# Attention sums over values: high and low parts in one product of six matmuls instead of nine

## The reference

```python
x = x + xattn(_layernorm(x), ctx)      # the part that is changed
x = x + ffn(_layernorm(x))             # top 2 of 8 experts and a shared one

q = (x @ Wq).reshape(b, n, HEADS, DIM_HEAD)
k = (context @ Wk).reshape(b, m, HEADS, DIM_HEAD)
v = (context @ Wv).reshape(b, m, HEADS, DIM_HEAD)
sim = jnp.einsum('bihd,bjhd->bhij', q, k) * SCALE
attn = jax.nn.softmax(sim, axis=-1)
out = jnp.einsum('bhij,bjhd->bihd', attn, v).reshape(b, n, HEADS * DIM_HEAD)
return out @ Wout + bout
```

## Time and profile before

| | |
|---|---|
| median of the timed runs | 1270.85 us |
| profiled execution | 1277.05 us |
| its span | 1275.4 us |
| granted TensorE clock, mean | 0.957 |
| TensorE busy | 1165.7 us (91%) |
| VectorE busy | 748.1 us (59%) |
| ScalarE busy | 671.6 us (53%) |
| GpSimd busy | 802.0 us (63%) |

### The profile page before, as it was taken

One profiled execution on the slowest core, in us unless ns is written; L12 is line 12 of the kernel. 1 busy time (PEld: TensorE's weight loads), 2 busy tenths in 40 slices (PEclk: granted clock), 3 DMA queues, 4 the chain that ended last, 5 costly groups with the idle time before them and its releaser, 6 DMA issues. The chain is left out here.

```text
span 1275.4 us, 27342 instructions
## 1 busy us (share of the span) xinstructions
PE 1165.7 (91%) x7710; PEld 1014.8 (80%) x7710; DVE 748.1 (59%) x2147; ACT 671.6 (53%) x1743; POOL 802.0 (63%) x867
## 2 busy tenths in 40 slices
PE   5989999999999999999998789996989999999792
PEld 4778888888888888888887678885878888888582
DVE  4667787778777877777777456565433333343231
ACT  4667776777677767776775342331233343433240
POOL 4778977897789778977897435654124444443241
PEclk9989999999999999999999689997999999999796
DMA  4213132213221322132214282212163354336634
GB/s 128 82 38 104 51 120 92 96 51 120 92 97 51 120 91 97 51 120 89 99 32 155 79 315 93 104 64 105 50 240 59 55 129 82 56 58 188 196 52 132
DMA packets 77104, 128.47 MB, mean 101 GB/s; under 512 B 18816, under 2 KB 63696, under 8 KB 72880
## 3 DMA queue, kind: packets, MB, share of 16 engines
q1 hardware_dynamic: 62256, 102.80, 23.9%
q0 software_dynamic: 14784, 24.84, 9.7%
HBM read 77.81 MB, written 53.48 MB: 103 GB/s over the span
## 5 line engine op out<-in xcount | busy, mean ns | idle before, releaser
L513 POOL TENSOR_TENSOR probs<-probs,inv_sum 112x375 f32<-112x375 f32 x256 | 208.9, 817 | 97.6 <-DVE inv_sum L742 97.6
L1186 POOL DMA_INDIRECT z_scratch<-stage,to_row x63 | 100.8, 1599 | 202.9 <-DMA z_scratch<-stage,to_row 102.6
L600 ACT ACTIVATE probs<-bank,neg_max 112x375 f32<-112x375 f32 x256 | 147.2, 575 | 126.7 <-DVE neg_max L730 123.5
L1432 DVE TENSOR_TENSOR hT_lo<-bank,hT_hi 128x512 fp32r<-128x512 f32 x91 | 62.9, 691 | 236.9 <-ACT hT_hi L1230 231.0
L730 DVE TENSOR_REDUCE neg_max<-bank 112x1 f32<-112x375 f32 x256 | 127.7, 541 | 32.5 <-PE bank L878 32.1
L907 PE MATMUL bank<-ident,probs 112*125 112x112 f32 x768 | 138.8, 291 | 7.7 <-POOL probs L513 7.7
L757 DVE TENSOR_TENSOR pT_lo<-bank,pT_hi 125x336 fp32r<-125x336 f32 x256 | 129.5, 506 | 27.1 <-ACT pT_hi L615 20.7
L907 PEld LDWEIGHTS bank<-ident,probs 112*125 112x125 f32 x768 | 107.2, 191 | 42.5 <-issue 24.4
L1224 ACT ACTIVATE stage<-bank 128x512 f32<-128x512 f32 x91 | 54.4, 598 | 154.9 <-PE bank L1496 152.7
L479 POOL TENSOR_TENSOR v_lo<-v_raw,v_hi 125x512 fp32r<-125x512 f32 x96 | 123.5, 1287 | 7.5
L615 ACT ACTIVATE pT_hi<-bank 125x336 fp32r<-125x336 f32 x256 | 113.4, 443 | 12.8 <-PE bank L907 12.8
(11 more groups left out here) (263 smaller groups left out, 3400.6 us busy)
## 6 DMA issues: line engine op xcount, KB each, us to landing
w_split_scratch<-stage SPq DMA_DIRECT2D x16, 1536.0 KB, 5.7
ring<-w_split_scratch SPq DMA_DIRECT2D x16, 1536.0 KB
stage<-in_L_ffn_W SPq DMA_DIRECT2D x48, 256.0 KB, 3.1
ctx_in<-in_ctx SPq DMA_DIRECT2D x32, 281.2 KB
xg<-x_sorted_scratch POOLq DMA_DIRECT2D x63, 136.0 KB, 3.5
x_in<-in_x SPq DMA_DIRECT2D x16, 224.0 KB, 4.0
x_res<-in_x SPq DMA_DIRECT2D x32, 112.0 KB, 3.1
x_scratch<-x SPq DMA_DIRECT2D x32, 112.0 KB, 1.9
```

What stands on the lines that cost most here:

```text
L513: pool.tensor_tensor(probs[:, s % 4, :], probs[:, s % 4, :], inv_sum[:, s:s + 1].to_broadcast([N, M]), ALU.mult).then_inc(probs_ready, 1)
L600: act.activation(probs[:, s % 4, :], S_BANK[s % 2][0:N, 0:M], ACT.Exp, bias=neg_max[:, s:s + 1], accum_out=row_sum[:, s:s + 1]).then_inc(e ...
L1186: pool.indirect_dma_start(out=z_dram[:, :], out_offset=bass.IndirectOffsetOnAxis(ap=to_row[:, j:j + 1], axis=0), in_=y_sb[j % 3], in_offse ...
```

## The change

The high and low parts of a head's values are put side by side in one tensor, v_both, 64 and 64 columns, and likewise the high and low parts of the transposed weights in pT, 112 and 112. One product of a head, 128 columns of values by 224 of weights, then holds in its quadrants high x high, high x low, low x high and low x low. For two heads and three pieces of context there are six matmuls, with 448 columns of O_BANK as result. The three quadrants that count have to be added, which the accumulation in PSUM did before: ScalarE copies low x high to o_cross (copy_cross), VectorE adds high x low to it (add_cross, into o_most), and then high x high for each head (add_most, into o_sum, an SBUF tensor). Only then come the high part (hi_of_o, ScalarE) and the low part (lo_of_o, VectorE), both from o_sum, one slot pair later than before. TensorE may write the bank again when o_sum is made, no longer when oT_lo is. wout of the even batch moves from slot 4 to slot 6 (that of the last batch too), since its inputs are made later, and the tail has two slots more.

```diff
-        ([], ["wout"]), ([], ["v2", "xt0"]), ([], ["xt1"]), ([], ["v1", "k3"])]
+        ([], []), ([], ["v2", "xt0"]), ([], ["xt1", "wout"]), ([], ["v1", "k3"])]
...
-        v_hi = [sb(f"v_hi{i}", [KR, KT, INNER], F32R) for i in range(2)]
-        v_lo = [sb(f"v_lo{i}", [KR, KT, INNER], F32R) for i in range(2)]
+        v_both = [sb(f"v_both{i}", [KR, KT, HEADS, 2, DH], F32R) for i in range(2)]
...
+        pT = sb("pT", [KR, 2, KT, 2, 2, N], F32R)
+        o_cross, o_most = sb("o_cross", [DH, 2, N]), sb("o_most", [DH, 2, N])
+        o_sum = [sb(f"o_sum{i}", [128, N]) for i in range(2)]
...
# ScalarE
+            def copy_cross(a):
+                act.wait_ge(o_made, a + 1)
+                act.activation(o_cross[:], o_parts()[64:128, :, 0, :], ACT.Copy).then_inc(cross_ready, 1)
+            def hi_of_o(a, j):
+                act.wait_ge(sum_ready, a + 1)
+                act.activation(oT_hi[j // 4][:, j % 4, :], o_sum[j % 2][:], ACT.Copy).then_inc(o_hi_ready, 1)
...
-                if s % 2 == 0 and not (first and s < 4):
-                    o_part(8 * p + s // 2 - 2, (s // 2 - 2) % 8)
+                if s % 2 == 0 and not (first and s < 6):
+                    hi_of_o(8 * p + s // 2 - 3, (s // 2 - 3) % 8)
+                if s % 2 == 0 and not (first and s < 4) and s < 20:
+                    copy_cross(8 * p + s // 2 - 2)
...
# VectorE
+            def add_cross(a):
+                dve.wait_ge(cross_ready, a + 1)
+                dve.tensor_tensor(o_most[:], o_parts()[:, :, 1, :], o_cross[:], ALU.add).then_inc(most_ready, 1)
+            def add_most(a, j):
+                dve.wait_ge(most_ready, a + 1)
+                for e in range(2):
+                    last = dve.tensor_tensor(o_sum[j % 2][DH * e:DH * e + DH, :], o_parts()[:, e, 0, :], o_most[:, e, :],
+                                             ALU.add)
+                last.then_inc(sum_ready, 1)
+            def lo_of_o(a, j):
+                dve.wait_ge(o_hi_ready, a + 1)
+                dve.tensor_tensor(oT_lo[j // 4][:, j % 4, :], o_sum[j % 2][:], oT_hi[j // 4][:, j % 4, :].bitcast(F32),
+                                  ALU.subtract).then_inc(o_ready, 1)
...
+                if s % 2 == 1 and not (first and s < 5) and s < 20:
+                    add_cross(8 * p + (s - 1) // 2 - 2)
+                if s % 2 == 1 and not (first and s < 7):
+                    lo_of_o(8 * p + (s - 1) // 2 - 3, ((s - 1) // 2 - 3) % 8)
+                if s % 2 == 1 and not (first and s < 5) and s < 20:
+                    add_most(8 * p + (s - 1) // 2 - 2, ((s - 1) // 2 - 2) % 8)
...
# TensorE
-                    wait(pe, o_ready, a)
-                    vh, vl, cols = v_hi[i], v_lo[i], slice(m * 128, (m + 1) * 128)
-                    pt = [t[:, j % 2, :, :, :].rearrange("p t e n -> p t (e n)") for t in (pT_hi, pT_lo)]
-                    product(O_BANK[:, 0:N2],
-                            [(v[:, kt, cols], w[:, kt, :]) for kt in range(KT)
-                             for v, w in ((vh, pt[0]), (vh, pt[1]), (vl, pt[0]))]).then_inc(o_made, 1)
+                    wait(pe, sum_ready, a)
+                    for e in range(2):
+                        for kt in range(KT):
+                            mm = pe.matmul(O_BANK[:, e * N2:(e + 1) * N2],
+                                           v_both[i][:, kt, 2 * m + e, :, :].rearrange("p l d -> p (l d)"),
+                                           pT[:, j % 2, kt, e, :, :].rearrange("p l n -> p (l n)"),
+                                           start=(kt == 0), stop=(kt == KT - 1))
+                    mm.then_inc(o_made, 1)
```

More of the change, by code:

```diff
@@ L475, in split_values @@
                 pool.wait_ge(unit_hi, n_hi)
-                pool.tensor_tensor(v_hi[b][:, t, :], v_raw[at_v][:], one[0:KR, :].to_broadcast([KR, INNER]),
+                raw = v_raw[at_v][:].rearrange("p (h d) -> p h d", h=HEADS)
+                pool.tensor_tensor(v_both[b][:, t, :, 0, :], raw,
+                                   one[0:KR, :].rearrange("p (o q) -> p o q", o=1).to_broadcast([KR, HEADS, DH]),
                                    ALU.mult).then_inc(v_hi_ready, 1)
                 pool.wait_ge(v_hi_ready, n_v)
-                pool.tensor_tensor(v_lo[b][:, t, :], v_raw[at_v][:], v_hi[b][:, t, :].bitcast(F32),
+                pool.tensor_tensor(v_both[b][:, t, :, 1, :], raw, v_both[b][:, t, :, 0, :].bitcast(F32),
                                    ALU.subtract).then_inc(v_ready, 1)
@@ L614, in slot @@
                     wait(act, o_made, 8 * p + t // 2 - 1)
-                    act.activation(pT_hi[:, (t // 2) % 2, :, t % 2, :],
+                    act.activation(pT[:, (t // 2) % 2, :, t % 2, 0, :],
                                    PT_BANK[t % 2][0:KR, 0:KT * N].rearrange("p (t n) -> p t n", t=KT),
@@ L633, in _ @@
             rounds(act, body)
-            for s in range(16, 19):
+            for s in range(16, 21):
                 slot(PAIRS - 1, True, s, False)
@@ L711, in _, with o_parts @@
                     unit(n + 1, name, 0, U_BANK[n % UNIT_BANKS])
+            def o_parts():
+                return O_BANK[0:DH, 0:2 * N2].rearrange("p (e l n) -> p e l n", e=2, l=2)
+            def add_cross(a):
[11 more added lines that the diff above has]
+                                  ALU.subtract).then_inc(o_ready, 1)
             def run(p, odd, last, name):
@@ L742, in slot @@
                     dve.reciprocal(inv_sum[:, s:s + 1], row_sum[:, s:s + 1]).then_inc(inv_ready, 1)
[L744 to L747, removed]
-                                      oT_hi[j // 4][0:64, j % 4, :].bitcast(F32), ALU.subtract)
-                    dve.tensor_tensor(oT_lo[j // 4][64:128, j % 4, :], O_BANK[64:128, N:N2],
-                                      oT_hi[j // 4][64:128, j % 4, :].bitcast(F32), ALU.subtract).then_inc(o_ready, 1)
+                if s % 2 == 1 and not (first and s < 5) and s < 20:
[4 more added lines that the diff above has]
+                    add_most(8 * p + (s - 1) // 2 - 2, ((s - 1) // 2 - 2) % 8)
                 for name in slots_of(p, odd, last)[s % 8][0] if lead else []:
@@ L756, in slot @@
                     dve.wait_ge(pT_hi_ready, gh - 1)
-                    dve.tensor_tensor(pT_lo[:, (t // 2) % 2, :, t % 2, :],
+                    dve.tensor_tensor(pT[:, (t // 2) % 2, :, t % 2, 1, :],
                                       PT_BANK[t % 2][0:KR, 0:KT * N].rearrange("p (t n) -> p t n", t=KT),
-                                      pT_hi[:, (t // 2) % 2, :, t % 2, :].bitcast(F32),
+                                      pT[:, (t // 2) % 2, :, t % 2, 0, :].bitcast(F32),
                                       ALU.subtract).then_inc(pT_ready, 1)
@@ L786, in _ @@
             dve.tensor_copy(first_logits[:], U_BANK[(n - 1) % UNIT_BANKS][:, 0:TC * 2 * E]).then_inc(unit_done, 1)
-            for s in range(18, 20):
+            for s in range(18, 22):
                 slot(PAIRS - 1, True, s, False)
```

11 lines of the change are left out of this document (4 added, 7 removed).

## The result

The changed kernel takes 1353.14 us (median of 4 runs, 1351.75 to 1356.53), the kernel before on the same chip 1271.22. The ratio is 1.065, with a 95% interval of 1.062 to 1.068: slower by 6.5%. The profiled execution took 1353.98 us, its span is 1352.4, the mean granted clock 0.945. The forecast was 1371: the median moved by 82 us where 100 had been forecast.

The account below looks back on a forecast made before the run. Two close limits a pair: TensorE about 42 us, the VectorE-ScalarE ring 38.33. Ring 38.33 + 0.8 + 9.5 = 48.6 against 42.53: 6.1 x 16 = 98, with tail 100, on 1270.85: 1371 us; 8-in-10 range 1262 to 1430.

Parts of the forecast that it names:

- The ring: Attention: VectorE and ScalarE wait for each other every two slots; 38.33 us a pair without TensorE before, 48.6 after.
- The second rival: GpSimd does not hold lo_of_o up: 1279 us, or 1266 with more overlap between the short adds; chance 0.13.
- the third: Attention: TensorE is the bound, VectorE's idle time takes up the added work, 43 us come out: 1228 us; chance 0.08.
- The fourth: Every round pays 2.02 us, as if GpSimd always has its next instruction ready: 1478 us; chance 0.12.
- The lock: Odd slots: lo_of_o, both operands in SBUF, waits for GpSimd, even past one boundary; a round +0.47 free, up to +2.02.
- The first rival: lo_of_o's wait ends with the running GpSimd instruction, so slots 5 and 7 cost 0.99 too: 1347 us; chance 0.15.
- Slot by slot: Added us by odd slot: even batch 0.99 in 1 and 3, 1.50 in 5, 2.02 in 7; odd batch 1.0 each.
- the toss-up: Slot 5, even batch: the next GpSimd instruction starts exactly where one ends, so lo_of_o may be passed over; 1.50 us taken.
- The moved output projection: wout from slot 4 to 6, 1.4 us: covered by the longer ring, otherwise only a moved wait; no net cost.
- The small terms: Durations of the added short operations: copy_cross 0.35, add_cross 0.38, add_most 0.26, hi_of_o 0.26 us.
- TensorE and its 43 us: Three fewer matmuls save 0.33 us a product, 43 us for 128, but appear nowhere since TensorE sets no round.
- A clock of 0.5 in the attention: Sign of being wrong: granted clock at 0.5; full clock was expected with TensorE busy 39 of 48 us.

Follow-up runs that it names:

- run 1: Changed kernel, but lo_of_o reads its first operand from O_BANK in PSUM, not from o_sum in SBUF; 1275.38 us, ratio 1.012 to the kernel before.
- run 2: Kernel before plus a spare VectorE subtraction in every odd slot, both operands in SBUF; 1307.83 us, ratio 1.040.
- run 3: Kernel before plus a spare VectorE subtraction in every odd slot, one operand in the PSUM bank; 1258.06 us, ratio 1.000.
- run 6: Kernel before with only the moved output projection (wout in slot 6, not 4; last batch likewise), nine matmuls; 1284.52 us, ratio 1.012.
- run 9: Changed kernel with lo_of_o and add_cross ahead of the odd slot's reciprocal on VectorE; 1281.05 us, ratio 1.010 to the kernel before.
- run 5: Changed kernel with nine matmuls a product again, three of them repeated; 1326.95 us, ratio 1.056 to the kernel before.
- run 4: Kernel before with six matmuls a product, low values times high weights left out; 1233.7 us, ratio 0.979.
- run 10: Changed kernel with the first half of GpSimd's value split using a full tile of ones, not a broadcast column; 1352.29 us, ratio 1.075 to the kernel before.
- run 11: As run 9, with wout of the even batch in slot 5, not 6; 1271.74 us, ratio 1.011 to the kernel before.
- run 12: As run 9, with v2 in slot 4 and wout in slot 5 of even batches; 1298.1 us, ratio 1.032 to the kernel before.

## Why the prediction was right

**The bound, and what the change adds to it.** Right. The ring's 48.6 us a pair stand against 48.4 in the two pairs above and 48.2 over pairs 4 to 14. The forecast added 100 us to the profiled execution, and 77 came (1353.98 against 1277.05). The 23 between them: 7 because the steady pairs grew by 5.68 us and not 6.1, 7 because the first and last pairs grew less than the steady ones (16 x 5.68 = 91 against 83.6), 1 because the tail of the attention grew by 1.2 us and not 2, and 8 because what stands behind that tail, in which nothing was changed, took 534.4 us after and 542.6 before.

The forecast's sum can also be split as run 1 splits it. The wait for GpSimd was to cost 9.5 - 8 x 0.47 = 5.7 us a pair, and costs 4.7 (48.27 - 43.53). All else was to cost 0.8 + 3.8 - 4.2 = 0.4, and costs 1.0 (43.53 - 42.53). One term was too large and the other too small, and the sum is nearer than its parts.

The second rival (no exclusion) and the third (TensorE the bound) fall by the same rows: lo_of_o is long, and the maxima wait for no scores. The fourth (2.02 in every round) falls by lo_of_o's median of 0.892.

**The lock, its size and its second half.** Right. lo_of_o at a mean of 1.03 us (forecast 0.8 to 1.3); 1.81 where it is passed over; run 1 takes the wait away and with it 5.3 of 6.5%. The Trainium skill ("SBUF — State Buffer", section "SBUF: two separate sides") has the exclusion, and runs 2 and 3 agree: a median of 0.624 us with two SBUF operands, 0.274 with one. It has it end with the running instruction, and the 32 cases that were passed over go against that. One row was misread on the way: in the earlier trace rows GpSimd was not quiet. In five of the six cases it was running an indirect DMA issue of 0.96 us (L1166), and the instruction took 0.193 us all the same. The comparison stands, and it shows that GpSimd does not hold VectorE up with every kind of instruction. The first rival, which rested on the same step, gave 1347 and so is nearer to 1353 than the forecast: its total is right by other errors that cancel, and it is the single instructions that decide against it.

**Slot by slot.** Partly right, with errors that cancel. What a slot of the even batch gained, forecast and measured: slot 1, 0.99 and 1.00; slot 3, 0.99 and about 0.4; slot 5, 1.50 and 2.22; slot 7, 2.02 and 1.93. Slots 3 and 7 are counted without the wait for scores that stood in them before (0.63 us), which the forecast had taken out too; between the exponentials slot 7 grew by 4.37 - 3.08 = 1.29 and slot 3 shrank by 0.26. The four add up to 5.5 us, forecast and measured. In the odd batch the odd slots grew by 0.7, 0.7, 1.3 and 0.8 us, 3.5 together, where 4.0 had been forecast. In slot 3 GpSimd runs only an operation on 112x2 elements beside lo_of_o, and it took 0.26 us there in 13 of 13 pairs: I had placed an L516 in every odd slot. In slot 5 the toss-up came out on the long side each time, since the normed x ahead of it also ends late (the reciprocal comes 1.01 us behind the exponential and not 0.70), and the last 0.3 of its 2.22 us are that.

**The moved output projection.** Right in its first half: in the changed kernel the long slot 5 covers it. Slot 4 falls from 2.88 to 1.59 us, and slot 6 grows only from 1.68 to 1.84. Wrong in its second: "if that cover is gone, the 1.4 us move a wait from slot 4 to slot 6 and cost nothing net". In run 6, which has no such cover, it costs 10 us, and slot 6 is at 2.40 and 2.34 us in runs 1 and 9, where the wait for GpSimd is gone or hidden. The wait in slot 4 was itself cover for VectorE's normed x, and I had taken the whole of it as saved.

**The small terms.** copy_cross 0.355 (0.354), add_cross 0.368 (0.381), add_most 0.263 (0.26). hi_of_o 0.306, where 0.26 was taken from its width. What such terms cost is less certain: I had counted nearly their whole duration, and run 3 has 0.27 us a round at no cost. But that is in the old ring, where waits for TensorE take them up; no run prices them in the changed one.

**TensorE and its 43 us.** "Nowhere" is right for the changed kernel, where nine matmuls in run 5 are no slower than six. In the old ring they are worth 21.9 us (run 4), 1.36 a pair, so TensorE had a part in the bound before, as its waits in the earlier trace rows said. "Near 80% in the attention, with waits for exponentials ahead of each score product" is wrong: 42.66 of 48.37 us is 88%, and the score products waited in 20 of 104 rounds. A clock of 0.5 in the attention had been named as a sign of being wrong, and it came:

```profile
347.00:350.40 3.40, 1.16 (x11) 0.72 (x9) 2.79 (x9) 2.83 (x10) 1.90 (x3) 1.00 0.61 179
350.40:353.80 3.40, 3.40 (x14) 3.40 (x15) 2.90 (x9) 1.62 (x5) 3.40 (x4) 0.50 0.23 64
353.80:360.00 6.20, 6.20 (x43) 5.38 (x42) 4.14 (x12) 4.11 (x12) 6.04 (x7) 1.00 0.00 0
```

TensorE was busy 1.16 of 3.40 us, since it waited 2.24 us for an exponential. For the next 3.4 us the granted clock was 0.50, that is 1.2 GHz. From 128 to 756 us there are eight such dips, of 3.4 or 6.8 us, in eight of 13 pairs; in the kernel before there was none from 85 to 699 us (the next is that of the earlier trace rows). The clock explains only part of TensorE's busy time. In the five pairs without a dip it was busy 40.90 to 41.47 us. The first line is one of them, the second a pair of run 1, with the same matmuls:

```profile
468.13:515.16 47.03, 40.90 (x280) 34.06 (x280) 40.58 (x105) 29.93 (x87) 35.71 (x38) 1.00 0.22 73
295.39:338.32 42.93, 39.72 (x281) 33.88 (x279) 35.19 (x105) 30.31 (x86) 35.02 (x39) 1.00 0.25 82
```

So a dip of 3.4 us adds about 1.5 us of busy time, and 1.2 us or more stay unexplained at the full clock. The dips cost little time: pairs without one take 47.88 us in the mean (47.03 to 48.96), pairs with one 48.50 (48.33 to 48.95), a difference of 0.6 of the 5.7 us. No run took the dips away alone, so even that is not shown to be their price.

**What the rest is made of.** Run 1 leaves 13.9 us in the attention. Run 6 accounts for 10.1 of loss and run 4 for 21.9 of gain; if these add up, the quadrant sums themselves cost 13.9 - 10.1 + 21.9 = 25.7 us, 1.6 a pair. That is a difference of runs on different chips and assumes that they add; it was argued and not measured. Run 3, where an added instruction cost nothing, speaks against simple adding.

## What to carry to other kernels

Before a product is rearranged to spare TensorE, ask from where the added sums read: a two-operand VectorE instruction that loses its PSUM operand can take four times its own duration while GpSimd works (1.03 us in the mean, against 0.26), and the profile shows it only as a long instruction, without idle time. Put such an instruction ahead of the one that releases GpSimd, as in run 9, or keep one operand in the bank, as in run 1. And before a step is moved out of a wait, look for what else that wait was hiding.

## What the runs showed of the hardware

- A VectorE instruction with two SBUF operands that waits for GpSimd is not always served when the running GpSimd instruction ends. With L516 and then L478 it was passed over 32 of 33 times (29 of them at 1.81 us), with the longer form of run 10 39 of 39 times (up to 2.06).
- Ahead of the first half of a value split, what went with it over seven traces was how early the split's input had been ready: 0.256 us or more before the boundary, passed over 140 of 140 times; 0.189 us or less, served 29 of 29. 39 of the 140 are of run 10's other form.
- That is not the whole rule. Ahead of the bias add on 112x256, whose input had been ready for 1.7 us or more, it was served 15 of 15 times in the changed kernel (0.77 to 0.81 us), but passed over once in run 9 and once in run 11 (1.26 and 1.10 us). Ahead of the first half of an expert's split, of the same form and with its input ready for 4.7 us, it was served 10 of 10 times in runs 9, 11 and 12. Ahead of an L516 it was served every time. What decides there stays open.
- Beside a GpSimd operation of 112x2 elements it did not wait: 0.26 us, 13 of 13.
- The normed x, a tensor by two columns of scalars from SBUF, waits for GpSimd and is passed over too (1.89 us, 15 times in run 12). Whether it is the scalars that make it wait, no run shows.
- A GpSimd instruction that issues an indirect DMA did not hold such an instruction up: 0.19 us beside it, 5 of 5 (kernel before, the rows behind the attention).
- On GpSimd the 128x112 subtraction takes 0.43 us, against 0.26 on an undisturbed VectorE.
